# First row of attention: the splitting of the query and output weights moved between engines and within a step

## What is computed

```python
q = (x @ wq_w.T + wq_b).reshape(b, t, 32, 32)          # x is layer-normalised
k = (x @ wk_w.T + wk_b).reshape(b, t, 1, 32)           # one shared key and value head
v = (x @ wv_w.T + wv_b).reshape(b, t, 1, 32)
scores = einsum('bqhd,bkd->bhqk', q, k[:, :, 0]) / sqrt(32), causal
attn = einsum('bhqk,bkd->bqhd', softmax(scores), v[:, :, 0])
x = x + attn.reshape(b, t, 1024) @ wo_w.T + wo_b
```

## Time and profile before

| | |
|---|---|
| time, median of 3 runs | 3070.78 us (3069.42 to 3071.02) |
| profiled execution | 3066.18 us |
| its span in the trace | 3064.4 us |
| mean granted TensorE clock | 0.949 of full speed |
| attention, of the 40 slices of 76.6 us | about 22 |
| TensorE busy | 2797.6 us (91%) |
| VectorE, ScalarE, GpSimd busy | 1635.2, 1166.0, 901.3 us |

### The profile page before, as it was taken

The page is one execution under the profiler, slowest core; times in us unless marked ns, Lnnn a source line. Parts: engine busy times, 40 slices in busy tenths (PEclk is TensorE's granted clock), DMA queues, the critical chain, the costliest instruction groups (busy, mean ns, idle before and its releaser), DMA issues. The chain is left out here.

```text
span 3064.4 us, 41835 instructions
## 1 busy us (share of the span) xinstructions
PE 2797.6 (91%) x15808; PEld 2128.5 (69%) x15808; DVE 1635.2 (53%) x2976; ACT 1166.0 (38%) x2509; POOL 901.3 (29%) x1444
## 2 busy tenths in 40 slices
PE   4788999999999999999999796999999999999988
PEld 3555767767767677677676555777777777777766
DVE  4454364454553645536435155666666666666653
ACT  2554264464562644636536012222222222222220
POOL 0112122122221221122312133535353535353522
PEclk9778999999999999999999887999999999999989
DMA  5555453545444545445444330010101020101011
GB/s 152 168 156 166 142 128 80 168 109 148 121 111 141 119 101 165 112 134 124 101 143 130 109 132 1 1 46 10 49 8 55 2 56 1 56 1 56 1 28 28
DMA packets 103626, 272.29 MB, mean 89 GB/s; under 512 B 12122, under 2 KB 23514, under 8 KB 101122
## 3 DMA queue, kind: packets, MB, share of 16 engines
q1 hardware_dynamic: 102512, 269.32, 32.2%
q10 hardware_dynamic: 914, 0.30, 0.0%
HBM read 168.40 MB, written 50.33 MB: 71 GB/s over the span
## 5 line engine op out<-in xcount | busy, mean ns | idle before, releaser
L512 DVE TENSOR_REDUCE top<-ps_attn 128x1 fp32r<-128x512 f32 (+3 forms) x704 | 438.6, 628 | 362.2 <-PE ps_attn L705 362.2
L339 POOL TENSOR_SCALAR_AFFINE_SELECT pt<-pt 128x512 f32<-128x512 f32 x256 | 163.6, 648 | 1075.7 <-ACT pt L409 1075.0
L423 ACT ACTIVATE spent<-ps_attn,top 128x512 f32<-128x512 f32 (+1 forms) x512 | 325.3, 635 | 337.6 <-DVE top L512 337.1
L1453 PE MATMUL ps_mixer<-m_w_hi,m_xt_hi 128*128 128x512 f32 x1024 | 415.6, 406 | 0.0
L409 ACT ACTIVATE pt<-ps_attn 128x512 f32<-128x512 f32 (+1 forms) x704 | 379.3, 556 | 75.4 <-PE ps_attn L732 73.4
L1454 PE MATMUL ps_mixer<-m_w_hi,m_xt_lo 128*128 128x512 f32 x1024 | 401.2, 392 | 0.0
L1455 PE MATMUL ps_mixer<-m_w_lo,m_xt_hi 128*128 128x512 f32 x1024 | 400.9, 392 | 0.0
L702 PE MATMUL ps_attn<-k_stack,q_stack 96*128 96x512 f32 (+3 forms) x1024 | 310.6, 356 | 93.1 <-ACT spent L423 63.3
L1120 ACT CAST m_xt_hi<-ps_mixer 128x512 fp32r<-128x512 f32 x192 | 104.2, 589 | 701.8 <-PE ps_mixer L1448 701.4
L732 PE MATMUL ps_attn<-q_stack,k_stack 97*128 97x512 f32 (+3 forms) x1024 | 297.0, 352 | 13.8 <-ACT pt L409 8.3
L702 PEld LDWEIGHTS ps_attn<-k_stack,q_stack 96*128 96x128 f32 x1024 | 180.5, 200 | 161.8 <-ACT spent L423 108.8
(11 more groups left out here) (216 smaller groups left out, 5149.7 us busy)
## 6 DMA issues: line engine op xcount, KB each, us to landing
xr<-in_a_x SPq DMA_DIRECT2D x64, 512.0 KB, 7.1
q_stack<-q_hi SPq DMA_DIRECT2D x128, 256.0 KB, 5.6
wq_hi<-wq_split SPq DMA_DIRECT2D x56, 512.0 KB, 3.8
wq_lo<-wq_split SPq DMA_DIRECT2D x56, 512.0 KB, 4.6
q_stack<-q_lo SPq DMA_DIRECT2D x64, 256.0 KB, 6.8
wo_hi<-wo_split SPq DMA_DIRECT2D x8, 2048.0 KB, 8.3
wo_lo<-wo_split SPq DMA_DIRECT2D x8, 2048.0 KB, 13.1
x<-xr SPq DMA_DIRECT2D x32, 512.0 KB, 2.8
```

The lines of the kernel that those rows point to most:

```text
L423: nc.scalar.activation(spent[:, 0:width], ps[:, S0 + n % 2, 0:width], ACT.Exp, scale=-1.0, bias=top[:, j * TILES + i:j * TILES + i + 1].bi ...
L512: nc.vector.tensor_reduce(out, ps[:, S0 + n % 2, 0:width * len(heads)].rearrange("p (j k) -> p j k", k=width), AX.X, ALU.min).then_inc(s_u ...
L1453: nc.tensor.matmul(out, a_hi, b_hi, start=first, stop=False)
```

## The change

The low parts of the query and output weights are made by GpSimd: wq_low at the head of its step, behind inv_sqrt and ahead of the first cut; wo_low behind the second cut. On ScalarE wq_high moves from behind the fourth row_sum to behind the first one (ahead of x_high(second, 2) in M = -2), and wo_high from behind the fourth exponential and sixth sum to behind the eighth exponential. The instructions, their operands and the semaphores that they raise stay the same; SP's and TensorE's programs are not edited.

```diff
--- before.py
+++ after.py
@@ -345,6 +345,19 @@
                     nc.gpsimd.tensor_tensor(at_lo[:, c, :], att[:, G % 2, :], at_hi[:, c, :].bitcast(F32),
                                             ALU.subtract).then_inc(olo_done, 1)
 
+                def wq_low(G):
+                    pool.wait_ge(wqhi_done, G + 1)
+                    nc.gpsimd.tensor_tensor(wq_lo[:, G % 2, :, :].rearrange("p c (d j) -> p c d j", j=GH),
+                                            wq_raw[:, :, :].rearrange("p c (j d) -> p c d j", j=GH),
+                                            wq_hi[:, G % 2, :, :].bitcast(F32).rearrange("p c (d j) -> p c d j", j=GH),
+                                            ALU.subtract).then_inc(wqlo_done, 1)
+
+                def wo_low(c):
+                    pool.wait_ge(wohi_done, c + 1)
+                    nc.gpsimd.tensor_tensor(wo_part(wo_lo, c).rearrange("p a m -> p (a m)"), bo_rows[:, :],
+                                            wo_part(wo_hi, c).rearrange("p a m -> p (a m)").bitcast(F32),
+                                            ALU.subtract).then_inc(wolo_done, 1)
+
                 def spread(G):
                     pool.wait_ge(den_inv_done, G + 1)
                     if G >= 2:
@@ -366,9 +379,13 @@
                     for t in range(TILES):
                         if (b := coming(M, 2 + t)) is not None and b:
                             inv_sqrt(pool, b, t)
-                    if inside(M):
-                        for k in range(TILES):
+                    if (G := wq_group(M)) is not None:
+                        wq_low(G)
+                    for k in range(TILES):
+                        if inside(M):
                             cut(M, k)
+                        if k == 1 and (c := wo_chunk(M)) is not None:
+                            wo_low(c)
                     for G in finishes(M):
                         finish_low(G)
                     if inside(M):
@@ -465,6 +482,8 @@
                         copy_rows(M)
                     if inside(M + 1):
                         row_sum(M + 1, 0)
+                    if (G := wq_group(M)) is not None:
+                        wq_high(G)
                     if second is not None:
                         x_high(second, 2)
                     if inside(M + 1):
@@ -476,11 +495,9 @@
                             exps(M, (u,))
                         if inside(M + 1):
                             row_sum(M + 1, u + 2)
-                        if u == 1 and (G := wq_group(M)) is not None:
-                            wq_high(G)
                         if u == 2 and inside(M + 2):
                             q_high(M + 2)
-                        if u == 3 and (c := wo_chunk(M)) is not None:
+                        if u == 7 and (c := wo_chunk(M)) is not None:
                             wo_high(c)
                         if u == 6 and first is not None:
                             x_high(first, 0)
@@ -559,19 +576,6 @@
                         dve.wait_ge(y_ready, Y_TILES * b + TILES * run + t + 1)
                         half = xr[:, n, (t % 2) * HALF:(t % 2 + 1) * HALF]
                         nc.vector.tensor_tensor(half, ps[:, (PROJ, MISC)[t % 2], :], half, ALU.add).then_inc(y_added, 1)
-
-                def wq_low(G):
-                    dve.wait_ge(wqhi_done, G + 1)
-                    nc.vector.tensor_tensor(wq_lo[:, G % 2, :, :].rearrange("p c (d j) -> p c d j", j=GH),
-                                            wq_raw[:, :, :].rearrange("p c (j d) -> p c d j", j=GH),
-                                            wq_hi[:, G % 2, :, :].bitcast(F32).rearrange("p c (d j) -> p c d j", j=GH),
-                                            ALU.subtract).then_inc(wqlo_done, 1)
-
-                def wo_low(c):
-                    dve.wait_ge(wohi_done, c + 1)
-                    nc.vector.tensor_tensor(wo_part(wo_lo, c).rearrange("p a m -> p (a m)"), bo_rows[:, :],
-                                            wo_part(wo_hi, c).rearrange("p a m -> p (a m)").bitcast(F32),
-                                            ALU.subtract).then_inc(wolo_done, 1)
 
                 for M in STEPS:
                     first, second = coming(M, 5), coming(M, 6)
@@ -590,16 +594,12 @@
                         tops(M + 1, (2, 3))
                     for b, t in tiles:
                         normalise(dve, b, t)
-                    if (G := wq_group(M)) is not None:
-                        wq_low(G)
                     if inside(M + 1):
                         tops(M + 1, (4,))
                     if inside(M + 2):
                         q_low(M + 2)
                     if inside(M + 1):
                         tops(M + 1, (5,))
-                    if (c := wo_chunk(M)) is not None:
-                        wo_low(c)
                     if inside(M - 1):
                         invert(M - 1, 0)
                     if inside(M + 1):
```

## The result

| | before | changed |
|---|---|---|
| time, median | 3070.1 us (3068.75 to 3071.02) | 3049.69 us (3043.5 to 3050.02) |
| profiled execution, span | 3066.18 us, 3064.4 | 3049.66 us, 3047.6 |
| mean granted TensorE clock | 0.949 | 0.957 |
| VectorE, ScalarE, GpSimd busy | 1635.2, 1166.0, 901.3 us | 1609.9, 1164.7, 943.1 us |

Both columns come from the same chip. The ratio is 0.9929, with a 95% interval of 0.9912 to 0.9946: 20.4 us faster by the medians. The forecast was 3041, with a range of 3018 to 3060.

A forecast was written before the change was run, and what follows sets the result against it. Weight casts and subtractions stopping the ring of scores, maxima and sums were the bound, with q_stack copies next. Gains in M = -1 to 6, less start, M = 8 and clock, summed to 29.5 us: 3041 us, range 3018 to 3060.

The forecast's parts named there:

- The bound: Steps M = 1 to 3: q_stack copies become the bound, 9.9 + 0.7 + 10.3 = 20.9 us (21.2 in M = 2 and 3).
- the ring: TensorE's scores, VectorE's maximum and ScalarE's sum over two banks; weight casts and subtractions stop it, some 10 us a step lost.
- Rival A: q_stack copies shrink from 10.3 to about 8 us, clock stays up; 51 us gained, 3020 us; chance 0.12.
- the sign that I named for the bound: At a step's start, first scores would wait 1 to 3 us for DMA q_stack.
- rival D: Low clock eats the gains, stalls return in part: 3063 to 3066 us, steps above 24 us; chance 0.06.
- The shift: 8 KB copy of maxima on SP, issued behind the output weight's transfers: stall of 0 to 1.5 us, taken as 0.7.
- Rival C: Shift late behind output weight's stores on SP: TensorE stalls 5.7 us in seven steps, 3076 us; chance 0.08.
- The start: M = -2: ScalarE's second query-weight cast waits for its raw load, so the first projection starts 5.1 us later.
- GpSimd's price: Low parts on GpSimd: 3.1 us for the strided query weight (2.39 to 4.8), 2.4 us for the contiguous output weight.
- Rival B: GpSimd needs 4.8 us or more for the strided part, making stack wait: 22 gained, 3049 us; chance 0.12.
- M = 8: Last output-weight store delays the 4 MB load in M = 7, so M = 8 is 2.3 us longer (0 to 3).
- The clock: Gaps at step starts may bring back TensorE's lower clock: 0.7 us in each of five steps, 3.7 us charged.

The follow-up runs named there:

- e1: Changed kernel with the output weight's stores and next load on SP moved behind the next step's shift: 3038.25 us, ratio 0.9890.
- e2: Changed kernel with wq_high back behind the casts of input tiles 2 and 3, in M = -2 only: 3041.78 us, ratio 0.9908.
- e7: Kernel before with only wq_high moved behind the first sum, all low parts still on VectorE: 3052.60 us, ratio 0.9952.
- e4: Changed kernel with only the query weight's part of the change, output weight split as in the kernel before: 3057.81 us, ratio 0.9954.
- e8: Changed kernel with the query weight's low part made twice on GpSimd: 3061.36 us, ratio 0.9977.
- e5: Changed kernel with only the output weight's part of the change, query weight split as in the kernel before: 3061.23 us, ratio 0.9955.
- e6: Kernel before with both low parts on GpSimd at the change's places, both high-part casts left where they were: 3061.32 us, ratio 0.9982.
- e3: Changed kernel with the edits of both e1 and e2: 3031.48 us, ratio 0.9873.
- e10: e3 with SP's q_stack copies ahead of the query weight's store and next raw load: 3034.11 us, ratio 0.9874.
- e11: e8 with SP's q_stack copies ahead of the store of the split query weight: 3065.23 us, ratio 0.9985.
- e9: Changed kernel with shift issued by ScalarE behind the copy of the rows, in all 64 groups, instead of by SP: 3104.78 us, ratio 1.0121.

## Why the prediction was right, and where it was off

**The bound.** "So taking the weights out of the ring can't give a step of 17.6 us: the q_stack copies become the bound." Right in part. No step from M = 1 to 5 got to 17.6, and M = 1 and 3 came out at 21.13 and 21.18 against 20.9 and 21.2. But the parts of that sum were off in opposite directions, and cancelled. Here are SP's timeline and the DMA's landing for M = 1.

```profile
110.63 1.21 SPq L292 DMA_DIRECT2D q_stack<-q_hi  x2
111.88 0.61 SPq L292 DMA_DIRECT2D q_stack<-q_lo  x1
```

```profile
q_stack<-q_lo SPq DMA_DIRECT2D x1, 256.0 KB, 6.7
```

q_hi ends at 110.61, the last copy lands at 111.88 + 6.7 = 118.6: **8.0 us, where the sum had 10.3**. I took M = 1 of before for it, where these copies went out close behind the weights' transfers. Now the query weight is stored and reloaded at 105.9 to 107.5, 3 us ahead, and the last of its transfers lands at 112.1, just after the last copy is issued. Rival A had this one term right. In return q_hi itself ends 12.1 us behind the step's first scores, where I had 9.9 from M = 11. That the total fits is luck. And the sign that I named for the bound, first scores waiting 1 to 3 us for q_stack, isn't there: behind M = 1 the copy lands at 118.6, just as TensorE has finished its other work, the first scores of M = 2, 3 and 5 don't wait at all and those of M = 4 wait 0.5 us. M = 2, at 25.4 us, also lies outside the 20 to 22.5 that I gave for M = 1 to 3, and above the 24 us that were to speak for rival D.

**The shift.** This is the step of the prediction that failed. It had the eighth exponential ending 14.8 us into the step and GpSimd's low part at 18.3, and from that "a stall of 0 to 1.5 us", with 0.7 in the sum. Here are ScalarE's row and GpSimd's row in M = 1.

```profile
115.75 1.05 ACT L477 CAST wo_hi<-bo_rows 128x1024 fp32r<-128x1024 f32 x1
```

```profile
116.88 2.38 POOL L357 TENSOR_TENSOR wo_lo<-bo_rows,wo_hi 128x1024 fp32r<-128x1024 f32 x1 [0.32 <-ACT wo_hi L477]
```

The step starts at 97.92, so the cast starts at 17.8 instead of 14.8, and the low part ends at 21.3 instead of 18.3. The durations were right (1.05 and 2.38 us); the 3 us come from the place of the eighth exponential. I read it from M = 11, a step at full clock with nothing late at its head. Here is how TensorE weighs at the head of M = 1, and of M = 11 of the kernel before:

```profile
99.36 1.94 PE L739 MATMUL ps_attn<-pt,v_sb 128*32 128x512 f32 x8
101.07 0.98 PE L739 MATMUL ps_attn<-pt,ones 128*32 128x256 f32 x8
```

```profile
395.02 1.06 PE L739 MATMUL ps_attn<-pt,v_sb 128*32 128x512 f32 x8
395.90 0.61 PE L739 MATMUL ps_attn<-pt,ones 128*32 128x256 f32 x8
```

The granted clock was 0.72 in the first 7 us of M = 1 and 1.00 in those of M = 11. From the first scores to the second ones it took 4.25 us instead of 2.73; the first scores came 0.9 us later against the copy of the maxima, one more short wait (0.43 us, for shift) stands behind; and the second sum starts 6.1 us into the step (104.01) instead of 3.7. The earlier trace rows had it at 5.0 us in M = 1 already. So the low part ended 0.2 us **behind** the step's end instead of 2.6 us ahead of it, and the three issues, which the forecast had finished by then, took their 2.4 us just as shift wanted to go. In M = 2, 4 and 5 the stall was 3.96, 3.35 and 3.30 us, in M = 3 2.07. Against the 0.7 in the sum that is 9.9 us over these four steps; M = 2, 4 and 5 fell short by 12.0 us together, and M = 3, with the smallest stall, not at all. e1 confirms it: with the order turned round, 11.4 us come back. Rival C had the right mechanism and place; its stall was to be 5.7 us in seven steps, with a landing 9.5 us after the issue, and was 2.1 to 4.0 in four of them (M = 2 to 5), with one after 3.7 to 5.5.

**The start.** 5.1 us later, said the sum. x_high(0, 2) starts at 37.80 instead of 31.97. Less the setup's 1.05 that is 4.8 us, and the chain is the predicted one, down to the instruction: ScalarE idles for the load of the second raw weight.

```profile
35.95 1.94 ACT L470 CAST wq_hi<-wq_raw 128x1024 fp32r<-128x1024 f32 x1 [5.42 <-DMA wq_raw<-in_a_wq_t]
```

The first projection starts at 41.82 against 36.00, so at 41 as said. M = -1 gained 3.8 (5.8 less the 2.0 by which M = 0 is late) against 2.6, inside its bounds of 0 to 4.2. e2 shows that most of the start's loss is exposed, 4.9 of 6.1 us.

**GpSimd's price.** Predicted 3.1 us (2.4 to 4.8) for the strided part and 2.4 for the contiguous one. Measured, by form over the whole span:

```profile
L350 POOL TENSOR_TENSOR wq_lo<-wq_raw,wq_hi 128x1024 fp32r<-128x1024 f32 x8 | 23.3, 2906 | 45.8 <-ACT wq_hi L470 45.8
L357 POOL TENSOR_TENSOR wo_lo<-bo_rows,wo_hi 128x1024 fp32r<-128x1024 f32 x8 | 19.0, 2376 | 9.2 <-ACT wo_hi L477 9.2
```

The stride costs GpSimd 0.53 us, VectorE 0.75 (1.98 against 1.23, rows 3) and ScalarE 1.03 (2.06 against 1.03, rows 2). Rival B is out. GpSimd is 1.9 times slower than VectorE on the contiguous operation and 1.5 times on the strided one. By the rule of the Trainium skill (GPSIMD Engine Reference, section 3.1 and the table in 4.1), elementwise work with two inputs belongs on VectorE; e7 against e4 bears this out so far that GpSimd gains nothing on the query weight, and e8 that a low part 2.9 us slower would have lost 12 us. "0.3 us late" in M = 2 to 4 wasn't seen: in M = 2 the low part ends at 127.8 and store_wq goes out at once, with q_hi still 7.6 us away.

**wq_high in idle time.** Right: in M = 1 it takes 1.99 us behind the first sum, and ScalarE still idles 1.14 us for the second maximum. No idle time of VectorE ahead of L529 is ended by a cast any more.

**M = 8.** The size was right (2.0 against 2.3), the mechanism wrong, so this term was luck. The last chunk's store was to hold the load back until 273; it didn't. load_first_wo went out 2.13 us into M = 7, and 2.14 us before the change. The last stores, issued at 243.3 and 243.7, landed in 2.8 and 3.8 us, not in the 7 that I took, so they were down at 247.5, 1.4 us into M = 7. What is longer is the landing of q_stack, and it varies with identical issue times in M = 7: 16.3 us before, 17.9 in the changed kernel, 19.1 in e5. e4, e6, e7 and e8 have M = 8 at 52.1 to 53.9 as well. Why is open. In e1 and e3, where load_first_wo really goes out later (5.8 us into M = 7), M = 8 takes 54.9 and 55.2 us, but in e10, with the same order, 53.2: that the mechanism costs 2 us once it acts is likely, not shown.

**The clock.** I charged 3.7 us for it, expecting that the gaps at the steps' starts would bring the lower level (1.2 GHz) back. Against the kernel before, the clock gave: its mean in M = 1 to 5 is 0.83 to 0.96 of full speed (2.4 GHz) where it was 0.75 or 0.76 in all five, and TensorE is busy for 96.4 us in these steps, 14.4 us less than before (110.8). But the sum was built from steps at full clock, and against these it took: TensorE is busy for 84.4 us in the counterparts without weights (16.6 four times and 18.0, rows 1), so 12.0 us longer here. Part of that lengthened the steps, as at the head of M = 1. Behind the stalls of 3.96, 3.35 and 3.30 us in M = 2, 4 and 5 the mean clock from 7 us into the step to its end was 0.78, 0.90 and 0.90; behind the 2.07 us in M = 3 it was 1.00. So the clock's term had its reason, but five times 0.7 make 3.5 us, not 3.7, and how much of the 12.0 us the steps really lost to the clock no run isolates.

**The sum.** 29.5 us were forecast, 20.4 measured by the medians, 20.7 at the start of M = 9. That is 8.8 us too high, and the stall of shift beyond its 0.7 us, 9.9 us over M = 2 to 5, is of that size. Without the clock's term the steps of the sum came to 33.2; of the 12.5 us by which these were too high, M = 2, 4 and 5 hold 12.0, their stalls 8.5 of these. The rest I can't divide: it is of the size of the clock's 3.7 us.

## What to carry to other kernels

When two casts and two subtractions interrupt a ring of three engines, first look for the idle time that the ring has anyway and move the cast there: one move of one instruction brought 15 of the 20 us here, and the second engine nothing measurable for that weight. When you compute whether something is ready before a small urgent DMA, take the time of its producer from the step that you are predicting, at its clock, and not from an undisturbed one (here 3 us, half of them the slower weighing at the step's head); and put the urgent copy ahead of bulk transfers in the queue's program, even if these then start one step later (e1). If two copies that somebody waits for share a queue with bulk transfers, an exchange of their order can move the stall from one to the other (e8, e11). And before you move a copy to another queue, ask what stood behind it in the old one (e9).

## What was not expected of the hardware

An 8 KB copy landed 1.8 to 2.1 us after its issue with nothing right ahead of it (M = 1 to 3 of the kernel before, M = 2 of e1), after 3.7 to 5.9 us behind 1.5 MB just issued on its queue (M = 0 to 6 of the changed kernel), and after 6.5 and 7.4 us with another 1.5 MB some 6 us further ahead (M = 2 and 1 of e11). Issued from ScalarE's queue instead, with SP's transfers under way, it took 6.2 us in M = 3 (e9): the way through another queue didn't pass them.

Two steps of the same work, M = 3 of the changed kernel and of e1, took 21.2 us with a stall of 2.1 us and a clock of 0.96, and 23.7 us with no stall and a clock of 0.79, TensorE being busy 18.0 and 21.8 us. Ahead of the slower one, in e1, TensorE had run M = 1 at 1.00 with 1.6 us idle in the whole step, and then M = 2 at 0.87; ahead of the other it had stood still for 4 us in M = 2. M = 3 of e10 had no stall either and took 22.2 us at 0.81, M = 4 20.8 us at 0.91. So the removal of a stall may bring less than its length, but these are single profiles, and what decides the clock of such a step stays open.
